# One bias product of 512 columns for two of 256, and a bank opened by its own first product, in an attention and spiking-MLP kernel

## The reference, cut to what matters

```
h = layernorm(x) * (1 + ca) + sa
q, k, v = (h @ W.T + b, split into 16 heads of 16)          # for Wq, Wk, Wv
s = q @ k.T / sqrt(16)
s = softmax of each 128x128 window of s under a causal mask (masked windows: 0)
p = softmax(s) over all 1024 keys
attn = (p @ v) @ Wo.T + Wo_b
x = x + ga * attn
h = layernorm(x) * (1 + cb) + sb
y = relu(h @ W_fc.T)**2 @ W_proj
x = x + gb * (spikes counted in 5 steps of a leaky integrator fed with y) / 5
```

## Time and profile before

| | |
|---|---|
| median of three executions | 2380.7 us (2380.19 to 2381.14) |
| the profiled execution | 2373.46 us |
| its span from first to last instruction | 2371.6 us |
| mean granted clock of TensorE | 0.993 |
| busy: PE, DVE, ACT, POOL | 94%, 74%, 65%, 48% of the span |
| PE matmuls in the trace | 19324 |

### The profile page before, as it was taken

The page is one execution under the profiler, slowest core; times in us unless marked ns, Lnnn a source line. Parts: engine busy times, 40 slices in busy tenths (PEclk is TensorE's granted clock), DMA queues, the critical chain, the costliest instruction groups (busy, mean ns, idle before and its releaser), DMA issues.

```text
span 2371.6 us, 46967 instructions
## 1 busy us (share of the span) xinstructions
PE 2220.5 (94%) x19324; PEld 1245.5 (53%) x19324; DVE 1750.9 (74%) x2113; ACT 1541.4 (65%) x2157; POOL 1137.5 (48%) x1070
## 2 busy tenths in 40 slices
PE   7889889999999999999999999999999999989988
PEld 4444344465545555455554555545554555545557
DVE  6787887768787676876778777776877767787456
ACT  2477676766667667675766766676666766667731
POOL 3153133545664456644666257653575544442630
PEclk8999999999999999999999999999999999999999
DMA  5233122211212113121133202231022211100000
GB/s 183 66 108 93 48 57 78 83 48 39 62 53 83 52 35 90 54 55 52 35 90 94 60 7 59 66 107 48 23 64 68 83 34 46 39 25 22 6 27 25
DMA packets 114066, 140.23 MB, mean 59 GB/s; under 512 B 8648, under 2 KB 86760, under 8 KB 113856
## 3 DMA queue, kind: packets, MB, share of 16 engines
q1 hardware_dynamic: 113856, 137.23, 20.4%
HBM read 74.26 MB, written 58.74 MB: 56 GB/s over the span
## 4 chain that ended last, share of the span: by engine, by line
PE 78%; DVE 9%; ACT 5%; POOL 4%; DMA 2%; issue 1%; SPq 0%; ACTq 0%; POOLq 0%
PE pv L799 11%; PE sums L789 9%; PE score L774 9%; PE ring L749 9%; PE score L719 8%; PE sums L731 8%; PE score L670 5%; PE score L687 4%; DVE e L1181 4%; PE ring L830 4%; DVE negmax L1159 3%; PE ring L752 2%; ACT e L1042 2%; PE score L777 2%; PE score L664 2%
## 5 line engine op out<-in xcount | busy, mean ns | idle before, releaser
L1042 ACT ACTIVATE e<-score 128x512 f32<-128x512 f32 x1152 | 672.2, 595 | 386.1 <-PE score L777 214.9
L1181 DVE TENSOR_TENSOR e<-ring,e 128x1024 f32<-128x1024 f32 x576 | 680.9, 1223 | 281.4 <-PE ring L830 281.0
L1159 DVE TENSOR_REDUCE negmax<-ring 128x8 f32<-128x1024 f32 x576 | 681.5, 1219 | 158.1 <-PE ring L752 147.2
L1047 ACT ACTIVATE e<-e 128x2048 f32<-128x2048 f32 x288 | 548.6, 1905 | 4.9 <-DVE e L1181 4.9
L774 PE MATMUL score<-q_st,k_st 112*128 112x512 bf16 (+3 forms) x1536 | 458.5, 330 | 56.3 <-ACT e L1042 23.7
L749 PE MATMUL ring<-k_st,q_st 96*128 96x512 bf16 (+3 forms) x1664 | 386.9, 317 | 38.8 <-DVE e L1181 18.4
L1486 POOL TENSOR_SCALAR r_p<-r_b,ab 128x256 bf16<-128x256 f32 x96 | 89.7, 934 | 548.7 <-DVE r_b L1187 548.7
L799 PE MATMUL pv<-e,v 128*17 128x512 f32 (+3 forms) x3072 | 311.4, 493 | 0.0
L789 PE MATMUL sums<-e,d_ones 128*32 128x256 f32 x4608 | 304.2, 382 | 1.5
L774 PEld LDWEIGHTS score<-q_st,k_st 112*128 112x128 bf16 x1536 | 147.8, 97 | 247.6 <-issue 120.7
L1465 POOL TENSOR_TENSOR gT<-gT 128x512 f32<-128x512 f32 x112 | 117.1, 1050 | 334.4 <-ACT gT L1015 334.4
(11 more groups left out here) (148 smaller groups left out, 2600.2 us busy)
## 6 DMA issues: line engine op xcount, KB each, us to landing
q_st<-q_parts SPq DMA_DIRECT2D x31, 768.0 KB, 5.9
k_st<-k_parts SPq DMA_DIRECT2D x31, 768.0 KB, 8.7
q_parts<-qk_p SPq DMA_DIRECT2D x30, 384.0 KB, 2.6
k_parts<-qk_p SPq DMA_DIRECT2D x28, 384.0 KB, 2.6
x_in<-in_x SPq DMA_DIRECT2D x8, 1024.0 KB, 5.7
q_parts<-qk_p SPq DMA_DIRECT2D x30, 256.0 KB, 2.9
x_res<-in_x SPq DMA_DIRECT2D x30, 256.0 KB, 4.1
k_parts<-qk_p SPq DMA_DIRECT2D x28, 256.0 KB, 2.9
```

The lines of the kernel that those rows point to most:

```text
L1042: act.activation(e[:, n % ES, hh, :], score[SCORE_SLOT["st", n, hh][0]][:, :], ACT.Exp, scale=DK ** -0.5).then_inc(e1_done, 1)
L1047: act.activation(v, v, ACT.Exp).then_inc(e2_done, 1)
L1159: dve.tensor_reduce(negmax[:, hh:hh + heads, at:at + NB // heads], slot[:, :].rearrange("p (h a n) -> p h a n", h=heads, n=P), AX_X, ALU.m ...
L1181: dve.tensor_tensor(v, ring[no % 2][:, :].rearrange("p (i n) -> p i n", i=2), v, ALU.mult).then_inc(ring_free, 1)
```

## The change

Three edits, all on the engines' own instructions. No table of the order is changed.

1. `tokens_by` issues the bias first, as one matmul of 512 columns with `start=True`, and all four fp32 products add to it. The column of ones is spread over all 128 partitions, where it was 3, and the moving operand is `b_out` with 128 rows, of which all but three hold zeros.
2. `mixed_products` no longer issues the four opening matmuls; the strip's own four products carry `start=True`. They write 256 of the bank's 512 columns.
3. `b_out` is `[128, 512]` bf16. VectorE clears it at the beginning, and writes the three rows twice, once for each half.

```diff
-        b_out = sb("b_out", [32, D], BF16)
+        b_out = sb("b_out", [P, 2 * D], BF16)
...
             def tokens_by(ps, src, n, w, bias=None):
+
+                if bias is not None:
+                    pe.matmul(ps, one[:, :].to_broadcast([P, P]), bias[:, :], start=True, stop=False, skip_group_check=True)
                 for i in range(2):
                     for k in range(NT):
                         mm = pe.matmul(ps[:, D * i:D * i + D], src[:, k, P * (2 * n + i):P * (2 * n + i) + P], w[:, k, :],
-                                       start=(k == 0), stop=(k == NT - 1 and bias is None))
-                    if bias is not None:
-                        mm = pe.matmul(ps[:, D * i:D * i + D], one[0:3, :].to_broadcast([3, P]), bias[0:3, :], start=False, stop=True)
+                                       start=(k == 0 and bias is None), stop=(k == NT - 1), skip_group_check=True)
                 return mm
...
                 pe.wait_ge(pv_evac, 2 * (m // NU) + 1)
-                for hh in range(QH):
-                    pe.matmul(pv[32 * hh:32 * hh + VW, :], id_b[:, 0:VW], mask_q[:, 0:1].to_broadcast([P, BANK]),
-                              start=True, stop=False, skip_group_check=True)
                 strip, c = columns(MIXED)[1]
-                strip_products(m, strip, c, False).then_inc(mixed_done, 1)
+                strip_products(m, strip, c, True).then_inc(mixed_done, 1)
...
             dve.memset(one[:, :], 1.0)
+            dve.memset(b_out[:, :], 0.0)
...
-            dve.tensor_tensor(b_out[:, :], b_a, b_h, ALU.add).then_inc(bias_step, 1)
+            for k in range(2):
+                ins = dve.tensor_tensor(b_out[0:3, D * k:D * k + D], b_a[0:3, :], b_h[0:3, :], ALU.add)
+            ins.then_inc(bias_step, 1)
             dve.memset(pv[:, :], 0.0).then_inc(bias_step, 1)
```

## The result

The changed kernel took 2359.46 us (median of four executions: 2357.05, 2358.39, 2360.53 and 5345.77 us), the kernel before 2380.44 us (median of four, 2376.25 to 2381.14). The last of the changed kernel's four was disturbed, and the ratio is formed without it: 0.9915, with a 95% interval of 0.9899 to 0.9931; the median of the other three is 2358.39 us. The forecast was 2359.0 us.

A forecast was written before the change was run, and what follows sets the result against it. TensorE was taken to bound the kernel (busy 94% of the span, 78% of the chain). Bias 16.5 us plus openings 5.2 us, beginning 0, gave 2380.7 - 21.7 = 2359.0 us; range 2352 to 2371 us.

The forecast's parts named there:

- The bias, 2.02 us a batch: Four bias pieces per batch on TensorE save 0.55 + 0.55 + 0.50 + 0.42 us; 14.1 over seven batches.
- The piece of 1.95 us: One full-height bias matmul, 0.23 us, then eight fp32 records, 1.72; the old piece took 2.50.
- Columns only: Rival: bias streams 512 columns either way, worth nothing; only the openings' 5.2 us remain, 2375.5 us; chance 0.07.
- Its fourth piece, 0.42 of 0.50: Batch's fourth bias piece: VectorE can come forward only by its two waits, 0.47 us less a handover.
- The last batch, 2.4 us: Two pairs of bias pieces in the last batch, each falling from 5.09 to 3.90 us, saving 1.2.
- The openings, 5.2 us: Mixed units: 0.22 us kept in 21 of 32 groups, 0.1 in six, nothing in five.
- the unit that comes from another piece: Six mixed groups where ScalarE arrives from another piece: 0.12 us gap, 0.1 counted each, 0.6 in all.
- The beginning, 0: VectorE's second writing of b_out delays the first maxima up to 0.6 us, then absorbed; ends 0 and +1 us.
- The sum: Whole kernel: 16.5 + 5.2 = 21.7 us saved; profiled execution 2373.46 to 2351.8, timed median 2359.0 us.
- the 7.2 us carried over: Timed median lies 7.2 us above the profiled execution, unexplained; carried over unchanged into the forecast.
- the clock: Rival: stretches at 1.2 GHz move or are added, up to 6.9 us each; cannot alone turn the sign; chance 0.04.
- Absorbed: Rival: TensorE waits instead; only first two pieces per batch and last pairs gain, 10.1 us, 2370.6 us; chance 0.12.

The follow-up runs named there:

- two tall matmuls: Kernel before, its two 256-column bias matmuls at their old places but 128 rows high instead of 3: 2364.87 us, ratio 0.9960.
- the single matmul in front: Kernel before with one 512-column bias matmul in front of the four products, still three rows high: 2375.43 us, ratio 0.9999.
- 64 rows: Changed kernel with the bias matmul 64 rows high instead of 128: 2372.36 us, ratio 0.9982.
- the hole filled: Four dummy 512-column matmuls in TensorE's wait for maxima at eight turns: kernel before 2375.9 us, without openings 2372.34, changed kernel 2355.55.
- the openings alone: Kernel before with only the four opening matmuls per group removed, the strip's own products carrying start=True: 2380.7 us, ratio 1.0017.

## Why the prediction was right, and where it was not

- **The bias, 2.02 us a batch.** 282.73 - 280.60 = 2.13 us with the openings gone, and 283.35 less 281.20 or 281.27, 2.15 or 2.08, with them in place. The piece of 1.95 us measured 1.94 and 1.95. The reading of the gap held: the height alone gives it (two tall matmuls, 2.00 us and -16.2 us), and without the height the single matmul in front gives less than half of it (0.25 us of 0.55). *Columns only* is refuted. A single low matmul between tall ones costs 0.30 us (2.30 against 2.00 from the product in front of it), two cost 0.25 each (2.55 against 2.06). The forecast counted gaps of 0.2 us in front of the bias; the trace shows them in front, behind and on the products that follow. The Trainium skill, "TensorEngine Tiling (Array Packing)", section "Key Properties", says that changing the tiling mode drains the engine. The gaps are of the kind that such a drain would leave, and 64 rows behave as 3 do; but no view names a mode, so that they are one is not shown. The Trainium skill, "TensorE: Matmul & The Clock Gate", section "Back-to-back issue gap", gives columns over clock plus 2.5 ns for a matmul taken by itself; by that one matmul fewer is worth 2.5 ns a piece. The runs disagree with it here: 0.56 us a piece was measured.
- **Its fourth piece, 0.42 of 0.50.** Third and fourth gave 1.02 us together where 0.92 was counted. The step that failed is a small one: TensorE's wait behind the fourth piece was to grow from 0.31 to 0.4, and fell to 0.19. From the piece's first start to VectorE's maxima it is 2.92 us now (972.39 to 975.31) and was 3.43 (976.22 to 979.65), 0.51 less, where the piece itself lost 0.50 (2.45 to 1.95). VectorE came forward by all of it, and the 0.05 us held back for a handover were not needed; the two waits of VectorE, 0.47 us, were gone altogether. TensorE's wait fell because 0.12 us of it moved: a few products ahead, from the tile's mask to the next scores, it is 0.25 us now (975.05 to 975.30) and was 0.13 (979.39 to 979.52). From the scores behind the piece to the end of the wait it is 2.25 us, and was 2.26.
- **The last batch, 2.4 us.** The pair that is shown saved 5.09 - 3.99 = 1.10 us, where 1.2 was counted, and the other 5.09 - 3.90 = 1.19; together 2.3. In the pair that is shown the second piece's products take 1.82 us to the start of the products of the values, weights of 17 columns, where those of the first take 1.73.
- **The openings, 5.2 us.** The comparison with the hole filled gives 3.6, and 3.9 at equal clock (0.992: 2376.04 us, five executions, to 2372.10, five). The bound of 0.22 us was right (0.20 kept at three of four units), but two of the steps behind the sum were wrong, in opposite directions. One unit of each batch was counted in full because ScalarE waits there; ScalarE's exponential does come earlier, but TensorE then stands in front of line 731. The question had been put to ScalarE alone, and VectorE holds that place. And the unit that comes from another piece was counted at 0.1 us, by a gap of 0.12 in the earlier trace rows; it gave 0.20. The gap understated the slack: ScalarE without openings, at the same place of the next batch,

```profile
1294.49 0.76 ACT L976 ACTIVATE hT<-score,modc 128x512 f32<-128x512 f32 x1
1295.16 2.51 ACT L1043 ACTIVATE e<-score 128x512 f32<-128x512 f32 x4
```

  starts the exponential 0.67 us behind an instruction of 0.76 us. Consecutive instructions of ScalarE overlap by about 0.1 us, so a gap of 0.12 us hides 0.2. Per batch 0.60 came out where 0.76 was forecast (3 x 0.22 + 0.1). With the bias part in place the openings give the same, 281.20 - 280.61 = 0.59.
- **The beginning, 0.** The second writing cost 1.22 us, the first maxima came 0.21 later, the second pair closed up, as the forecast had it. The long stretch at the lower clock took 10.2 us where it had 13.8, but that is not the change's doing: in the second profiled execution of the changed kernel it takes 13.7 us (41.7 to 55.4, clock 0.52).
- **The sum.** A batch shrank by 283.33 - 280.60 = 2.73 us, forecast 2.78. The nearness is in part luck, since the bias gave 0.11 more than its 2.02 and the openings 0.16 less than their 0.76. Over seven batches and the ends, it is 20.4 us with the hole filled in both kernels and 21.7 at equal clock, against 21.7.
- **The clock, and the 7.2 us carried over.** This is where the forecast of the profiled execution missed, and where the median's hit is partly luck. The profiled execution of the kernel before had a mean clock of 0.993, at which this kernel takes 2373.61 us (21 executions), and the timed ones took what it takes at 0.990, 2379.86. So the unexplained difference was, by all signs, the clock. (That is inferred from the relation; the clock of those three executions is not on record.) The changed kernel's executions were at 0.990 too, profiled one and timed ones, so 21.7 us below 2380.7 was what they showed. Its profiled execution has six stretches at the lower clock that the profiled one of before lacks, at 94.6, 176.5, 296.0, 364.2, 992.3 and 1555.5 us, at some 1.7 us each, 10.2 us (an estimate for the four of the beginning, since 1.7 is measured on the two in the middle); the first stretch, 3.6 us shorter at half speed, gives back up to 1.8. That leaves 8.4, of the size of the 6.6 by which it missed its own forecast of 2351.8. On the third chip, where the kernel before ran at 0.9915 in the mean, the change was worth 2376.71 - 2358.28 = 18.4 us, 3.3 less than forecast; 1.9 us times the 1.5 thousandths between the two clocks is 2.9 of it. So the step of carrying the 7.2 us over unchanged came out because both sets of timed executions ran at 0.990, the kernel before's as inferred. The rival *the clock* did not turn the sign for the whole change, but the clock outweighed one half of it alone, 1.0017 with an interval above 1.
- **Absorbed.** It asked for 10 us that TensorE waits more, and a kernel of 2370.6 us. Neither is there: what TensorE's busy time leaves of the span was 151.1 us and is 150.4.

What stays open: which kernels and executions get the stretches. The kernel with the bias part alone, openings in place, had the same mean clock as the changed kernel (0.9895 and 0.990), and the one with the openings alone a lower one (0.9868); but two tall matmuls (0.9887), one low one in front (0.9871) and 64 rows (0.9877) lie below the kernel before (0.9914 and 0.9917 on their chips) too, so the stretches cannot be laid to the openings or the bias alone. In the beginning every trace has a long stretch from 41 to 45 us on, in two of them in two parts, and a short one at about 72 us; between 90 and 370 us there are none to four, in the changed kernel four in one execution and none in another. Stretches from 2090 us on are in every trace. No run filled the waits in front of these.

Open too is what other low matmuls cost. The spreading of the inverse sums (`ring<-r_p,sel`) has weights 32 rows high and stands among products of 128 and 112 rows in each of the 288 units; no run tried it at full height.

## What to carry to other kernels

A small matmul among large ones is not priced by its columns: if its weights fill fewer rows than those of its neighbours, look at the idle time in front of its weight load, and try it at full height with zeros in the unused rows, which here was worth 16 us of 2380 for no less computation. When a step comes earlier, ask each engine that the next matmuls wait for, not only the one that visibly waits, what its own chain hangs on. And when a removal makes a kernel slower, or two executions differ, compare at equal mean clock first: a wait once per batch can cost more in clock than the removed work gave (2380.7 us, against 2372.34 with the wait filled). A few matmuls that compute nothing in it can win that back, but only where the clock does fall: in the kernel before four did nothing, and six cost 4 us.

## What the runs showed of the hardware

- A bf16 matmul of 3 or of 64 rows among products of 128 rows costs 0.30 us more than one of 128 rows, equally for both heights (2.30 us each, against 2.00 from the product in front of it). Products of 112 rows stand next to those of 128 without it: 0.23 us from the 512 columns of one to the next start.
- The mean granted clock explains most of the spread of this one-core kernel: 1.7 to 1.9 us for each 0.001, 2382 to 2372 us from 0.988 to 0.994. The lower level, 1.2 GHz, comes back behind a wait of 1.52 us followed by one of 0.80, in some executions and not in others, and each such stretch costs 1.7 us; four matmuls of 512 columns in the first of the two waits kept the clock at 2.4 GHz there in the profiled execution of each of the three kernels that had them.
- Two writings of 3x256 elements by VectorE took 2.55 us while GpSimd was at work, hardly less each than one of 32x256 elements (1.33 us).
